# Swin block in fp32: values, projection and the MLP's second product load 128 tokens as one weight instead of two times 64

## The reference

```python
h = _ln(x, ln1_g, ln1_b)
win = _window_partition(jnp.roll(h, (-s, -s), axis=(1, 2)), w)
q, k, v = jnp.split(win @ qkv_w + qkv_b, 3, axis=-1)          # then split into heads
attn = softmax(q @ k.T * hd ** -0.5 + rel_pos_bias + shift_mask)
out = (attn @ v).reshape(nB, N, C) @ proj_w + proj_b
x = x + roll(window_reverse(out), (s, s))
h2 = gelu(_ln(x, ln2_g, ln2_b) @ fc1_w + fc1_b) @ fc2_w + fc2_b
return x + h2
```

## Time and profile before

| | |
|---|---|
| runs | 501.56, 503.25, 504.86 us; median 503.25 |
| profiled execution | 500.17 us, of it a span of 498.4 us |
| TensorE matmul busy | 436.9 us, 88% |
| VectorE, GpSimd, ScalarE busy | 383.7, 378.2, 294.9 us (77, 76, 59%) |
| TensorE's granted clock, mean | 0.985 of full speed |
| attention stage, first to last step | about 34 to 346 us |
| MLP stage | about 347 to 493 us |

### The profile page before, as it was taken

One profiled execution on the slowest core, in us unless ns is written; L12 is line 12 of the kernel. 1 busy time (PEld: TensorE's weight loads), 2 busy tenths in 40 slices (PEclk: granted clock), 3 DMA queues, 4 the chain that ended last, 5 costly groups with the idle time before them and its releaser, 6 DMA issues.

```text
span 498.4 us, 21474 instructions
## 1 busy us (share of the span) xinstructions
PE 436.9 (88%) x9630; PEld 329.1 (66%) x9630; DVE 383.7 (77%) x549; ACT 294.9 (59%) x437; POOL 378.2 (76%) x376
## 2 busy tenths in 40 slices
PE   0665978899999899999999999787999999999995
PEld 0542756687777777777777767675566676667664
DVE  2767697889999999899999989965467766777652
ACT  1233665675765665666657646543777677767761
POOL 2658989988988989989889799730588888888830
PEclk9995999999999999999999999999999999999999
DMA  8300523511411511511111101100011321330333
GB/s 166 68 1 22 130 64 69 122 30 26 118 34 26 125 29 24 130 25 27 41 26 35 35 24 31 39 3 3 3 40 49 87 59 30 87 78 11 87 90 81
DMA packets 9986, 27.10 MB, mean 54 GB/s; under 512 B 3368, under 2 KB 3368, under 8 KB 7976
## 3 DMA queue, kind: packets, MB, share of 16 engines
q1 hardware_dynamic: 9896, 25.74, 22.0%
HBM read 9.21 MB, written 8.39 MB: 35 GB/s over the span
## 4 chain that ended last, share of the span: by engine, by line
PE 71%; DMA 9%; ACT 8%; SPq 4%; issue 4%; DVE 2%; ACTq 0%; DVEq 0%
PE work L697 26%; PE outs L697 17%; PE scores L697 16%; DMA kX<-kT 5%; PE scores L798 5%; ACT kT L610 4%; PE scores L838 4%; SPq L283 3%; DMA params<-in_params 2%; ACT qT L612 2%; PE work L712 2%; DMA x<-in_x 1%; PE outs L826 1%; ACT probsT L645 1%; SPq L275 1%
## 5 line engine op out<-in xcount | busy, mean ns | idle before, releaser
L373 POOL TENSOR_TENSOR probs<-probs,negmax 128x1024 f32<-128x1024 f32 x64 | 123.8, 1934 | 27.2 <-DVE negmax L489 27.1
L339 POOL TENSOR_TENSOR stat_rstd<-stat_var,minus_half 128x8 f32<-128x8 f32 (+1 forms) x62 | 104.9, 1691 | 5.0
L483 DVE TENSOR_TENSOR probs<-scores,bias 128x1024 f32<-128x1024 f32 x64 | 77.9, 1217 | 14.2 <-PE scores L697 14.2
L645 ACT ACTIVATE probsT<-scores 128x1024 f32<-128x1024 f32 x64 | 65.6, 1025 | 28.8 <-PE scores L798 28.8
L344 POOL TENSOR_TENSOR xn<-x,stat_mean 128x256 f32<-128x256 f32 (+1 forms) x91 | 78.1, 876 | 4.1
L697 PE MATMUL outs<-vX,probsT 128*64 128x34 f32 x2048 | 72.2, 225 | 9.4 <-issue 8.3
L489 DVE TENSOR_REDUCE negmax<-probs 128x16 f32<-128x1024 f32 x64 | 78.1, 1220 | 2.2
L697 PEld LDWEIGHTS outs<-vX,probsT 128*64 128x64 f32 x2048 | 65.9, 138 | 19.1 <-issue 19.0
L697 PEld LDWEIGHTS work<-params,probs 128*64 128x64 f32 x2048 | 62.3, 138 | 23.5 <-DVE x L577 20.5
L798 PEld LDWEIGHTS scores<-ident,probs 128*128 128x128 f32 x512 | 55.5, 142 | 28.1 <-issue 24.2
L610 ACT ACTIVATE kT<-work,bqkv 128x512 f32<-128x512 f32 x31 | 21.3, 688 | 86.6 <-PE work L697 86.6
(11 more groups left out here) (61 smaller groups left out, 662.4 us busy)
## 6 DMA issues: line engine op xcount, KB each, us to landing
kX<-kT SPq DMA_DIRECT2D x124, 64.0 KB, 2.0
x<-in_x SPq DMA_DIRECT2D x32, 224.0 KB
out<-x SPq DMA_DIRECT2D x28, 224.0 KB
x<-in_x SPq DMA_DIRECT2D x32, 32.0 KB
out<-x SPq DMA_DIRECT2D x28, 32.0 KB
out<-x SPq DMA_DIRECT2D x16, 56.0 KB
params<-in_params SPq DMA_DIRECT2D x1, 805.5 KB, 12.0
out<-x SPq DMA_DIRECT2D x16, 8.0 KB
```

Source lines behind the costliest of these rows:

```text
L339: nc.gpsimd.tensor_tensor(stat_rstd[:, cols], stat_var[:, cols], minus_half[:, cols], ALU.pow).then_inc(ln_rstd, pieces)
L373: nc.gpsimd.tensor_tensor(e, e, top, ALU.add).then_inc(shifted, 1)
L483: nc.vector.tensor_tensor(e[:, :].rearrange("q (u a m) -> q a u m", u=2, a=2), scores[k].rearrange("q (a u m) -> q a u m", a=2, u=2), b.re ...
L645: nc.scalar.activation(probsT[n % 2][:, :], trans, ACT.Exp)\
```

## The change

In V, Y and fc2 each weight was half of 128 neighbouring tokens, and its result went to partitions 0 to 63 or 64 to 127 of the bank. Now the whole 128 tokens are one weight, and the result goes to all 128 partitions. The loops over the two halves fall away. The moving operand, the results, their places in PSUM and all waits stay as they are.

```diff
                 elif kind == "V":
                     for wi in range(4):
-                        for p in range(2):
-                            at = i * IMG + wi * P + p * N
-                            for w in range(2):
-                                rows = slice(C * w, C * (w + 1))
-                                done = mm(work[w][N * p:N * (p + 1), wi * C:(wi + 1) * C],
-                                          xT[of % 2][rows, at:at + N], wqkv[rows, 2, C * w:C * (w + 1)])
+                        at = i * IMG + wi * P
+                        for w in range(2):
+                            rows = slice(C * w, C * (w + 1))
+                            done = mm(work[w][:, wi * C:(wi + 1) * C],
+                                      xT[of % 2][rows, at:at + P], wqkv[rows, 2, C * w:C * (w + 1)])
                 elif kind == "Y":
...
                     for c in range(WIN):
-                        for half in range(2):
-                            at = (WIN * i + c) * P + half * C
-                            for p in range(2):
-                                rows = slice(C * p, C * (p + 1))
-                                done = mm(work[p][C * half:C * (half + 1), c * C:(c + 1) * C],
-                                          oT[of % 2][rows, at:at + C], proj[rows, :])
+                        at = (WIN * i + c) * P
+                        for p in range(2):
+                            rows = slice(C * p, C * (p + 1))
+                            done = mm(work[p][:, c * C:(c + 1) * C],
+                                      oT[of % 2][rows, at:at + P], proj[rows, :])
...
                 for k in range(4):
                     for w in range(2):
-                        to = (2 * k + w) * C
+                        to, at = (2 * k + w) * C, w * BANK + k * P
                         for half in range(2):
-                            for part in range(2):
-                                at = w * BANK + k * P + part * C
-                                done = mm(work[s % 2][C * part:C * (part + 1), to:to + C],
-                                          hidden[s % 2][half][:, at:at + C], w2[:, half, :],
-                                          start=half == 0, stop=half == 1)
+                            done = mm(work[s % 2][:, to:to + C],
+                                      hidden[s % 2][half][:, at:at + P], w2[:, half, :],
+                                      start=half == 0, stop=half == 1)
```

## The result

The kernel became slower: 563.14 us (561.88 to 564.11, 4 runs) against 502.98 (501.56 to 504.86, 4 runs), a ratio of 1.122 with an interval of 1.117 to 1.127. The profiled execution took 564.11 us with a span of 562.3, against 500.17 and 498.4. In a few kernels some executions lie more than 1.5% above the fastest of the same kernel; ratios leave these out wherever they occur.

The account below looks back on a forecast made before the run. TensorE bounds the kernel, wholly in the MLP and partly in attention, paced by weight loads. fc2 50.2, Y 11.7 and V 2.3 us sum to 64 us more, giving 566 us (own range 558 to 574, wider 553 to 578).

Parts of the forecast that it names:

- The pace is the weight load's, whatever moves: In V, Y and fc2, weight-load time, not moving columns, sets the interval between starts: 58 ns for 64-column weights.
- A full fp32 weight loads in 108 to 109 ns, taken at 110 a start: New 128-row by 128-column weights in V, Y and fc2: load 108 to 109 ns, one start every 110 ns.
- the bounds of 107 and 114: Low and high ends, in ns, for the interval between starts with the new weights; worth -3 and +4 us in all.
- The load lies under the matmul before it: In fc2, a weight load overlaps the running matmul although both use the same 128 rows; about 55 ns within 58.
- the third rival: Load and matmul come in turn in fc2, Y and V: 163 ns a start, 651 us in all; chance 3%.
- fc2: 3.52 us from first to last start, 1.56 more a turn: MLP's second product: first to last start 3.52 us instead of 1.87; 1.56 us more per turn after a 0.09 saving.
- The saving at the transposes: Between fc2 and the transposes behind it the change of array shape falls away: 0.09 us saved, 29 times.
- Y: 0.81 more, uncovered but for 1.3 us: Attention stage: each Y block takes 0.81 us more; waits in five loop Y hide 1.3 us; 11.7 us in all.
- V: covered by the exponentials but for 0.08 us: Attention stage: V takes 0.41 us more, 0.33 hidden behind ScalarE's exponentials; 0.08 left in 30 of 32 V, 2.3 us.
- Nothing else changes: Other engines' work behind the longer blocks, DMA and waits for spread keys: costed at nothing; full granted clock expected to hold.
- the terms for V and Y: Attention stage: 2.3 us for V and 11.7 us for Y; 10.7 us from third to last V.
- fc2's 50 us: MLP: fc2's longer blocks, all on the path, 29 x 1.56 + 3 x 1.65 = 50.2 us more.

Follow-up runs that it names:

- the trace with the fillers: Changed kernel plus one 512-column matmul into a free bank before each of the last two Y and after them: 559.55 us, ratio 1.119 to the kernel before.

## Why the prediction was right

It said 566 within 553 to 578, and 64 us of difference; measured are 563.1 and 60.2 (63.9 in the profiled executions). Step by step:

- *The pace is the weight load's, whatever moves.* Right, shown by 32, 64 and 128 moved columns, at 112 ns each.
- *A full fp32 weight loads in 108 to 109 ns, taken at 110 a start.* It is 112 a start, inside the bounds of 107 and 114.
- *The load lies under the matmul before it.* Right; the third rival, at 163 ns, is out.
- *fc2: 3.52 us from first to last start, 1.56 more a turn.* 3.51 and 1.56, with a first step of 0.16 and 30 of 0.112 where the prediction had 0.22 and 30 of 0.110. The saving at the transposes is 0.09 us as forecast, but half in another place: they start 0.11 us behind fc2's last start, not 0.06 (0.04 saved), and their own block is 0.05 shorter (0.60 busy against 0.66); their first load now starts 0.11 us ahead of the first transpose, where it started with it before.
- *Y: 0.81 more, uncovered but for 1.3 us.* Right in the rows: 1.93 us to `score` is 0.84 more, 0.79 in the block (1.73 us from first to last start) and 0.05 in the change of shape behind it. Alone it costs 11.5 us in the profiled execution and 15.3 by the medians; its trace has a low stretch of the clock at the MLP's start too, 6.8 us long.
- *V: covered by the exponentials but for 0.08 us.* Right, 0.07.
- *Nothing else changes.* Wrong twice, with opposite signs. The attention loop grows by 3 us less than the terms for V and Y say; torn blocks and the waits for the spread keys are candidates, and I had read V's 0.96 us to `weigh` without looking at the V that took longer. And the granted clock is at half for 10.2 us at the start of the MLP instead of 3.4, which costs 3.4 us by the trace with the fillers, where the kernel before loses at most 1.5 (34.9 against 33.4 us). The prediction put both at nothing. That the total fits to 4 us is partly luck; that fc2's 50 us fit is not.

What stays open: why some instruction packets come late, so that blocks stand still. Fewer instructions around them helped, and where in the loop they are dense was not tried by itself. Nor is it settled how much of the 3 us in the attention loop the torn blocks explain.

## What to carry to other kernels

For fp32 matmuls with few moving columns count slots, not instructions. A slot is the time between two starts in the same part of the array's columns. It lasted about as long as the longer of one weight's load (its columns) and the moving columns: 112 ns for 128-column weights, 58 for 64, and for 32-column weights 56 ns with 64 moved columns and 36 with 34. Parts of the array's columns fill side by side, so the narrower weights, each going to its own part of the PSUM partitions, win until load and move are equal. By the same working a full-width weight would draw level where 128 columns move; no run here has halves with 128 moved columns. Before shortening the slots further, look in the timeline for blocks that are torn in two with "issue" between them, and compare them with the times of the instruction packets: there the supply of instructions limits, not the array.

## What the runs showed that I had not expected

- TensorE lost its clock while it was busy without a gap: with 32 moved columns under each 128-column load the granted clock was 0.50 from 397 to 414 us, and the kernel was 65 us slower than with 64 moved columns, for less arithmetic.
- Twice the moved columns are nearly free under a full fp32 weight: 3.56 against 3.51 us for the block.
- A `weigh` of 64 short matmuls stood still for up to 4.2 us in its middle, and the shorter slot made the whole kernel 2.9% slower. All 61 such stops of over 0.5 us ended 1.22 to 1.62 us after an instruction packet landed.
